# Causal attention of layer 1: masking the exponentials by key with a minimum on VectorE, in place of mask products on TensorE

## The reference, cut to what matters

```
h = rmsnorm(x, ln1_w)
q, k, v = heads(h @ wq.T), heads(h @ wk.T), heads(h @ wv.T)
q = q * cos + rotate_half(q) * sin        # k likewise; k, v repeated for 4 heads
scores = einsum('bhtd,bhsd->bhts', q, k) / sqrt(16)
scores = where(tril(ones(T, T)), scores, -1e30)
att = softmax(scores, axis=-1)
x = x + einsum('bhts,bhsd->bhtd', att, v) -> (B, T, C) @ wo.T
flat = rmsnorm(x, ln2_w)                  # then router probabilities, the 2 best of 8 experts
```

## Time and profile before

| | us |
|---|---|
| median of 3 timed runs (lowest, highest) | 4176.56 (4174.68, 4178.3) |
| the profiled execution, its own time | 4173.4 |
| its span, first to last instruction | 4171.6 |
| PE busy | 3724.6 (89%) |
| DVE busy | 2822.9 (68%) |
| ACT busy | 2307.4 (55%) |
| POOL busy | 1969.3 (47%) |
| mean granted PE clock | 0.926 |

### The profile page before, as it was taken

One profiled execution on the slowest core, in us unless ns is written; L12 is line 12 of the kernel. 1 busy time (PEld: TensorE's weight loads), 2 busy tenths in 40 slices (PEclk: granted clock), 3 DMA queues, 4 the chain that ended last, 5 costly groups with the idle time before them and its releaser, 6 DMA issues.

```text
span 4171.6 us, 110110 instructions
## 1 busy us (share of the span) xinstructions
PE 3724.6 (89%) x31697; PEld 2593.0 (62%) x31697; DVE 2822.9 (68%) x9352; ACT 2307.4 (55%) x5677; POOL 1969.3 (47%) x2276
## 2 busy tenths in 40 slices
PE   7499947697999889999898769999999999899999
PEld 7366624485666656666687546666666666555555
DVE  2488849685888744444465778888888887455554
ACT  5455525322444434444343547888888888455555
POOL 0144438674565422222375655566556655343433
PEclk9999977797999999999855879999999999899999
DMA  2111124331111233333111220000000001333332
GB/s 54 35 34 34 33 44 114 85 83 37 36 39 37 61 75 77 79 81 81 45 39 40 64 66 10 12 12 12 14 13 12 12 12 29 78 72 78 72 80 57
DMA packets 465512, 203.02 MB, mean 49 GB/s; under 512 B 435090, under 2 KB 455566, under 8 KB 465170
## 3 DMA queue, kind: packets, MB, share of 16 engines
q1 hardware_dynamic: 465298, 200.65, 21.3%
HBM read 154.67 MB, written 45.91 MB: 48 GB/s over the span
## 4 chain that ended last, share of the span: by engine, by line
PE 73%; DVE 10%; issue 6%; POOL 5%; SPq 2%; DMA 2%; ACT 1%; DVEq 0%; POOLq 0%; ACTq 0%
PE att_pS L3694 6%; PE att_pP L3707 6%; PE att_pO L3726 5%; PE sw_pH L4208 5%; PE moe_pH L2744 5%; PE sw_pY L4195 5%; PE moe_pY L2767 4%; PE moe_pH L2748 3%; PE att_pS L983 2%; DVE att_M L1193 2%; PE moe_pH L2754 2%; PE att_pQ L3667 2%; PE att_pS L2237 1%; PE att_pO L1045 1%; PE ret_pR L1854 1%
## 5 line engine op out<-in xcount | busy, mean ns | idle before, releaser
L3593 POOL TENSOR_TENSOR att_P<-att_P,att_rden 125x498 f32<-125x498 f32 x512 | 509.6, 1016 | 384.9 <-DVE att_rden L3899 384.9
L3790 ACT ACTIVATE att_P<-att_Z,att_nb 125x249 f32<-125x249 f32 x1024 | 499.3, 493 | 10.5 <-DVE att_nb L3911 10.5
L2809 DVE TENSOR_TENSOR moe_hT<-moe_silu,moe_pH 128x498 f32<-128x498 f32 x384 | 258.8, 674 | 310.9 <-ACT moe_silu L2793 310.9
L3911 DVE CUSTOM_DVE_ANT_0 att_Z<-att_pS,att_mask 125x249 f32<-125x249 f32 x1024 | 380.4, 409 | 104.6 <-PE att_pS L3694 87.8
L4256 ACT ACTIVATE sw_hT<-sw_pH,sw_b 128x498 f32<-128x498 f32 x512 | 317.9, 672 | 220.1 <-PE sw_pH L4208 220.1
L2793 ACT ACTIVATE moe_silu<-moe_pH 128x498 f32<-128x498 f32 x384 | 225.1, 586 | 261.8 <-PE moe_pH L2748 176.0
L2720 POOL TENSOR_TENSOR moe_xe<-moe_share,moe_x 128x1992 f32<-128x1992 f32 x32 | 130.0, 4064 | 428.4 <-DMA moe_share<-mixing 392.1
L4115 POOL TENSOR_TENSOR sw_acc<-sw_acc,sw_Z 128x249 f32<-128x249 f32 x224 | 154.0, 688 | 364.2 <-DVE sw_Z L4335 363.4
L3797 ACT ACTIVATE att_PTr<-att_pP 125x996 f32<-125x996 f32 x256 | 255.8, 999 | 123.9 <-PE att_pP L3707 116.9
L3694 PE MATMUL att_pS<-att_kT,att_qT 64*125 64x249 f32 x2048 | 284.7, 396 | 25.9 <-DVE att_nb L3911 25.7
L3707 PEld LDWEIGHTS att_pP<-att_ident,att_P 124*125 124x125 f32 (+1 forms) x2048 | 244.3, 189 | 88.6 <-issue 88.6
(11 more groups left out here) (463 smaller groups left out, 9636.0 us busy)
## 6 DMA issues: line engine op xcount, KB each, us to landing
moe_share<-mixing SPq DMA_DIRECT2D x64, 498.0 KB
sw_share<-mixing SPq DMA_DIRECT2D x64, 498.0 KB, 5.6
ffn_W<-in_ffn_pairs SPq DMA_DIRECT2D x64, 192.0 KB, 2.4
att_F<-h_stream SPq DMA_DIRECT2D x192, 62.5 KB
att_X<-h_stream SPq DMA_DIRECT2D x192, 62.5 KB
h_stream<-att_H SPq DMA_DIRECT2D x64, 62.5 KB
ffn_F<-h_stream SPq DMA_DIRECT2D x64, 62.5 KB
ret_F<-h_stream SPq DMA_DIRECT2D x64, 62.5 KB
```

The source lines that it names most:

```text
L2809: v.tensor_tensor(hT[:, u, k, :, :], sl[:, k % 3, :, :], pH[:, k % 3, :, T:2 * T], ALU.mult).then_inc(*hid_ready.one())
L3593: g.tensor_tensor(own, own, bc(rden[:, j % 2, c, :], T), ALU.mult).then_inc(*scaled.one())
L3790: ins = a.activation(P[:, r, c, t, :], Z[:, r, c, t, :], ACT.Exp, scale=-1.0, bias=nb[:, r, c, t:t + 1], accum_out=den[:, r, c, t:t + 1])
L3911: ins = v.tensor_tensor_reduce(Z[:, s % 2, c, t, :], pS[:, c, t * T:(t + 1) * T], mask[:, u, s // HP, t, :], -1.0, -TAKEN, ALU.add, ALU.mi ...
```

## The change

The products of `mask_key` are taken out; its wait stays, in `free_key`. The products by key start their own group. DVE gets a constant tile `limit` of 125 x 250 f32, 3.0e38 where a key may be seen and 0 where it may not, and in the odd steps takes the minimum of the exponentials with it, in place, over the 2 x 250 columns of the diagonal blocks of two heads. A new event `masked` counts these; PE waits for it, in place of `exp_ready`, before the products with V. In DVE's queue the minimum of d = 0 stands in step 1 behind `add_max` of the other half, that of d = 1 in step 3 ahead of the rotation L2456, that of d = 2 in step 5 ahead of the rotation L2459, and that of d = 3 in step 7 behind L2509 and ahead of `add_max` of pair n. The mask by query stays on PE.

```diff
-        mask16 = st.sb("mask16", [PT, 2, 2, PT], BF16)
+        mask16 = st.sb("mask16", [PT, 2, PT], BF16)
+        limit = st.sb("limit", [PT, 2, PT])
...
-            def mask_key(n, d):
+            def free_key(n, d):
                 pe.wait_ge(*exp_ready.after(n, d - 1))
-                for side in range(2):
-                    pe.matmul(pS[:, side, 0:2 * PT], ident16[0:PT, 0:PT],
-                              mask16[:, 1, :, :].rearrange("p t k -> p (t k)"), start=True, stop=True)
...
                 return pe.matmul(pS[:, side, out], kT[r:r + ROOM, u, b, k], qmT[r:r + ROOM, b, q],
-                                 start=False, stop=True, tile_position=(r, 0), skip_group_check=True)
+                                 start=True, stop=True, tile_position=(r, 0))
...
-                    mask_key(n, d)
+                    free_key(n, d)
...
-                    pe.wait_ge(*exp_ready.after(n))
+                    pe.wait_ge(*masked.after(n))
...
-            for way in range(2):
-                v.tensor_copy(mask16[:, way, :, :], bcm(mask[:, way, :], 1, 2))
+            v.tensor_copy(mask16[:, :, :], bcm(mask[:, 0, :], 1, 2))
+            v.tensor_scalar(limit[:, :, :], bcm(mask[:, 1, :], 1, 2), 0.0, 3.0e38, ALU.is_equal, ALU.mult)
...
             def main(n, u, step):
                 if step == 1:
                     add_max(n, u, 1)
+                if step % 2 == 1:
+                    d = step // 2
+                    hd = 2 * (1 - d % 2)
+                    own = EX[:, u % 2, d // 2, hd:hd + 2, 0:2 * PT]
+                    v.wait_ge(*exp_ready.after(n, d))
+                    v.tensor_tensor(own, own, bcm(limit[:, :, :].rearrange("p t k -> p (t k)"), 1, 2),
+                                    ALU.min).then_inc(*masked.one())
```

More of the change, by code:

```diff
@@ L57 @@
     "att1.const_loaded": 11,
+    "att1.masked": 4,
     "att1.exp_ready": 4,
@@ L2018, in stage_attention1 @@
         names = """xg_ready x_ready xT_done xT_ready r_done rot_ready q_ready k_ready v_done v_ready s_done max_ready
-            m_done qm_ready st_done exp_ready o_done OT_ready turned den_ready of_ready back oT_ready y_done x2_ready
+            m_done qm_ready st_done exp_ready masked o_done OT_ready turned den_ready of_ready back oT_ready y_done x2_ready
             h_ready fl_ready flT_done flT_ready l_done l_top l_shifted l_exp compared ranked rank_ready vec
@@ L2022, in stage_attention1 @@
         (xg_ready, x_ready, xT_done, xT_ready, r_done, rot_ready, q_ready, k_ready, v_done, v_ready, s_done, max_ready,
-         m_done, qm_ready, st_done, exp_ready, o_done, OT_ready, turned, den_ready, of_ready, back, oT_ready, y_done,
+         m_done, qm_ready, st_done, exp_ready, masked, o_done, OT_ready, turned, den_ready, of_ready, back, oT_ready, y_done,
          x2_ready, h_ready, fl_ready, flT_done, flT_ready, l_done, l_top, l_shifted, l_exp, compared, ranked,
@@ L2217, in mask_query @@
                     pe.matmul(pS[:, 2 + side, OFF:LOW], ident16[0:PT, 0:PT],
-                              mask16[:, 0, :, :].rearrange("p t k -> p (t k)"), start=True, stop=True)
-            def mask_key(n, d):
+                              mask16[:, :, :].rearrange("p t k -> p (t k)"), start=True, stop=True)
+            def free_key(n, d):
                 pe.wait_ge(*exp_ready.after(n, d - 1))
-                for side in range(2):
-                    pe.matmul(pS[:, side, 0:2 * PT], ident16[0:PT, 0:PT],
-                              mask16[:, 1, :, :].rearrange("p t k -> p (t k)"), start=True, stop=True)
             def by_query(n, u, d, side, t):
```

## The result

The changed kernel takes 4266.86 us (median of 4 runs, 4265.9 to 4267.37). The kernel before took 4175.62 in the same comparison (4 runs, 4170.78 to 4178.3): ratio 1.022, 95% interval 1.0202 to 1.0237. The forecast was 4217, its range 4192 to 4240. The sign was right; the loss is 91 us where 41 were worked out.

A forecast was written before the change was run, and what follows sets the result against it. The prediction took DVE to bound stretch A, POOL and PE stretch B; +0.93 and +0.47 us a slot over 27 slots, plus 3.2 us, made +41 us, so a median of 4217 us, range 4192 to 4240.

The forecast's parts named there:

- A: Slot stretch from DVE's maxima of d0 to d2, 7.54 us, bound by DVE; two unheld minimums add 0.93 us.
- The rival that PE is the bound: DVE's spare 2.7 us take the minimums and 0.57 us a slot come back, 15 us: 4161; 5%.
- The set-up: One of two casts becomes a two-operation tensor_scalar behind a wait for constants: nothing, at most 0.3 us.
- The clock falls: Rival: PE's busy share in a slot drops from 92% to 79%, clock to 0.77; 11 us more, 4228; 8%.
- B: Slot stretch from d2 to the next d0, 6.71 us, bound by POOL and PE; claimed to grow by 0.47 us.
- worth nothing: Removing d3's and d0's mask products, in B ahead of kT where PE waits anyhow, gains nothing.
- the rival's second price: Falling clock, case where PE then also ends A: 4245 us; the rival as a whole had 8%.
- 1.3 us of PE behind kT: PE's part of B after kT, which a clock of 0.77 would lengthen by 0.4 us.
- neither was held, so the chain DVE, power, kT does not move: In B, d2's minimum starts about with POOL's norm power; claimed neither is lengthened, so the chain costs nothing.
- The rival that names this: In B, d2's minimum holds the norm's power some 0.5 us, kT with it: 13.5 us, 4231; 10%.
- the held minimum of d3: In B, starts mid-kT, is held until kT ends, delays the add L2450 and PE's d0 products: +0.47 us.
- The sum: +0.93 + 0.47 = +1.40 us a slot, 37.8 us over 27 slots, plus 3.2 us in four earlier slots: +41 us.

The follow-up runs named there:

- Experiment 6: Changed kernel, each minimum replaced by a one-SBUF-input reduction (no mask by key), plus six filler products on PE ahead of d0: 4206.58 us, ratio 1.0076.
- experiment 4: Changed kernel without the minimums, so no mask by key at all, neither products nor minimums: 4199.69 us, ratio 1.0056.
- 7: Changed kernel with no mask by key at all, plus six filler products on PE ahead of d0: 4168.53 us, ratio 0.9984.
- 8: Kernel before, with only d2's mask products replaced by a minimum, placed behind the add L2450; products stay for d0, d1, d3: 4170.31 us, ratio 0.9989.
- 3: Changed kernel plus the filler: six bf16 products on PE ahead of d0's products, read by nothing: 4224.37 us, ratio 1.0122.
- experiment 1: Changed kernel with the mask products by key put back beside the minimums, so the mask is applied twice: 4248.61 us, ratio 1.0187.
- Experiment 2: Changed kernel, each minimum replaced by a same-length reduction with one input from SBUF; mask by key left out: 4244.99 us, ratio 1.0171.
- experiment 5: Changed kernel with six filler products ahead of d0 and the minimum of d3 moved behind the add L2450: 4211.67 us, ratio 1.0089.

## Why the prediction was wrong

**Right: A is DVE's, +0.93 us.** Experiment 6 measures 0.92 in A with the clock held and POOL left alone. The unheld minimum takes 0.67 us in its row, as the nearest row had it; what removing the products is worth was put, ahead of experiment 4, at 0.25 us a slot at most, and experiments 7 and 8 give 0.18 and 0.20. The rival that PE is the bound is refuted: with no minimum at all and the clock held, 7 us come back, not 15. The set-up cost nothing (the row of the new two-operation form shows 0.28 us).

**Wrong first, and largest: "The clock falls", put at 8% and at 11 us, and at nothing in the sum.** The step that failed is its argument: the mean busy share of a slot beside that of two windows of 100 us. The mean says nothing here. In after PE is busy 87% of the 24 slots (products at half clock count for longer) and the clock is 0.85; with the filler it is busy 85% and has 1.00. In after the sparse stretch of a slot, in which PE does little (0.81 us of 2.37), stands ahead of every fall: the falls of the 24 slots come from 0.3 us before its end to 0.9 us behind it. That stretch was known. It is the end of B, where the prediction called d3's and d0's mask products "worth nothing", since PE waits there anyhow. They were worth nothing on the chain and they were what kept PE at work while it waited. Experiment 4 shows that by their removal alone, 3 and 7 by putting work of no use back. Priced over the 26 full slots that the maxima of d0 mark off: 1.13 x 26 = 29 us; the rival's second price, 4245 "if PE then ends A too", 28 us more than forecast, was near. The second half of the miss is where the price falls: the prediction let the slow clock stretch 1.3 us of PE behind kT, but it lasts 6.8 us, through the projections and the products with V (L2303 567 ns on the mean), so that PE comes late for the add too and A grows by 0.62 us, in which PE was thought to have room.

How the runs line up bears this out, and shows where it stops. In the sparse stretch PE works 1.37 to 1.59 us in the kernel before and 1.39 to 1.51 with the filler, without a fall in the 24 slots; 1.09 to 1.42 in experiment 1, where 10 of the 24 have a long A; 1.16 in 4, where 7 have; 0.81 in after, where 18 have. But within after, 1 and 4 the same stretch stands ahead of slots with and without a fall: what decides for the single slot was not found.

**Wrong second: "neither was held, so the chain DVE, power, kT does not move".** It moves by 0.36 us a slot (power 1646 to 2006 ns). The pair of rows that this rested on, the power of the dense experts beside L1694, has the other order: there POOL's power was under way at 621.59 when DVE's operation came at 622.00; here DVE's minimum starts 0.17 us ahead of the power. In after both orders stand: with a minimum that starts inside the tail's power neither is longer; with one that starts ahead of the norm's power the power is. The two powers differ in size too (4 and 8 elements a partition), so that the order alone does it is not shown. But the trace of before had the nearer pair, with DVE's two-input operation first and POOL's the longer for it (0.81 us, where the same operation took 0.61 in the slots without the ranking):

```profile
1196.53 0.41 DVE L2534 TENSOR_TENSOR att_over<-att_over,att_ties 125x256 f32<-125x256 f32 x1
...
1196.60 0.81 POOL L642 TENSOR_TENSOR att_norm_centered<-att_F,att_norm_sum 125x256 f32<-125x256 f32 x1 [1.96 <-DVE att_norm_sum L637]
```

The rival that names this had 10% and 0.5 us.

The Trainium skill ("SBUF — State Buffer", section "Who interferes with whom") has a DVE instruction with two SBUF inputs contend with any GpSimd instruction that reads SBUF, and the order of issue decide who is held. Experiment 2 agrees: with one input, 1646 ns again. The tail's power does not: the minimum of d0 came second and still took 0.67 us. How much of the minimum's last 0.50 us the power stood still for, the rows don't tell; it grew by 0.36.

**Mis-sized: the held minimum of d3, "near 1".** It takes 1.44. The prediction had it start 4.88 us after d2, 0.84 into kT, and need 0.53 us behind kT. In the rows of after it starts 4.55 us after d2 (1207.15), 0.16 into kT, and needs 0.54 behind kT's end: the hold was rightly seen, and it is longer because kT comes 0.35 us later and DVE gets there 0.33 sooner. In B the hold was worth +0.47; experiment 5, which takes the minimum out of the way of the add, gives back 0.32 (7.39 to 7.07). The other 0.36 of B's growth (6.71 to 7.07) is what the power grew by, so the hold adds only what reaches beyond the later kT. Together they are 0.69 where 0.47 stood.

**The sum.** The 26 slots from the sixth maximum of d0 on grew by 72.2 us (26 x 2.75 = 71.5), where 27 x 1.40 = 37.8 stood (26 x 1.40 = 36.4); the five slots ahead of them grew by 10.8 us in all, where 3.2 stood, and the first maximum of d0 came 1.55 us earlier: together the 81.5.

**Open.** 12.1 us arise behind the last slot's d0. Some 3.5 of them are in the stage's drain; most of the others, 8.6, are in the attention of layer 3, which was not edited. From that d0 to the end the single profiles took 2749.6 us (before), 2761.8 (after), 2757.8 (1), 2763.6 (2), 2762.2 (3), 2758.6 (4), 2757.0 (5), 2758.7 (6), 2752.1 (7) and 2754.2 (8), while the kernel before varies by 13 us over its 21 runs. No experiment was aimed at it.

## What to carry to other kernels

An instruction that "hides in a wait" may be what an engine's clock lives on: before work is taken off PE, look at the stretch of the slot in which PE will then wait, not at its mean share, and ask what stands behind it at half speed. A two-input operation of DVE on SBUF is put where POOL is idle or where neither is on the path; moving one minimum by one place in the queue was worth 0.32 us a slot here. To weigh whether a neighbour holds another, take rows with the same order of start and the same size, not only the same kinds of instruction.

## What was not expected of the hardware

- Taking 256 products away made the kernel 0.56% slower, and six products a slot that nothing reads made the changed kernel some 41 us faster (some 30 us without the minimums).
- The clock stood at 0.50 for 6.8 us after a stretch in which PE worked 0.81 of 2.37 us; its longest idle time there was 0.71 us, just ahead of the products at 1212.84.
- A power over 8 elements a partition, 1.65 us long, was stretched to 2.01 by a minimum that started 0.17 us ahead of it and overlapped it for 0.50; another that came into a power 1.02 us long changed neither.
- A minimum that met kT and then POOL's next operation took 1.44 us, and that operation went from 0.61 to 1.05: both pay.
